# Where the normalised rows are transposed: on TensorE, or on the DMA queue of SyncE

## What is computed

```python
def _layernorm(x, axis=-1, eps=1e-05):
    m = jnp.mean(x, axis=axis, keepdims=True)
    v = jnp.var(x, axis=axis, keepdims=True)
    return (x - m) / jnp.sqrt(v + eps)

# attention: q = LN(x) @ w_q, k = ctx @ w_k, v = ctx @ w_v, causal softmax(q k^T / sqrt(512)) @ v
x = x + jnp.tanh(g_xattn[0]) * _L0_xattn_ref(_layernorm(x, axis=-1), ctx_1024, ctx_1024, w_q, w_k, w_v, 1)
# net: h = gelu(LN(x) @ ternary(W1)^T + b1), h @ ternary(W2)^T + b2
x = x + jnp.tanh(g_ffn[0]) * _L0_ffn_ref(_layernorm(x, axis=-1), W1, b1, W2, b2)
```

## Time and profile before

| | |
|---|---|
| measured, median of 3 | 1773.13 us |
| span of the profiled execution | 1771.6 us |
| TensorE matmuls busy | 1716.0 us, 97% |
| VectorE busy | 903.2 us, 51% |
| ScalarE busy | 784.0 us, 44% |
| GpSimd busy | 307.7 us, 17% |
| transposes L831 | 1024, in 128 sets of 8 |
| ScalarE copies of a set (L464, L509) | 128, about 1.02 us each |

### The profile page before, as it was taken

The page is one execution under the profiler, slowest core; times in us unless marked ns, Lnnn a source line. Parts: engine busy times, 40 slices in busy tenths (PEclk is TensorE's granted clock), DMA queues, the critical chain, the costliest instruction groups (busy, mean ns, idle before and its releaser), DMA issues.

```text
span 1771.6 us, 27014 instructions
## 1 busy us (share of the span) xinstructions
PE 1716.0 (97%) x10048; PEld 911.8 (51%) x10048; DVE 903.2 (51%) x1639; ACT 784.0 (44%) x1160; POOL 307.7 (17%) x341
## 2 busy tenths in 40 slices
PE   5799999999999999889999999999999999999999
PEld 2466656665666666555444444444444444444444
DVE  4565666666656665778443343334334434344332
ACT  2334343433343345433445544454545544554443
POOL 1111111111111111122111211122112211121110
PEclk8899999999999999999999999999999999999999
DMA  4112121121212144332110011101110111101100
GB/s 172 60 49 84 49 90 43 53 91 36 97 48 91 41 137 150 106 134 94 37 48 25 23 47 47 47 0 47 47 47 0 47 47 47 34 13 47 48 25 24
DMA packets 44570, 105.17 MB, mean 59 GB/s; under 512 B 5328, under 2 KB 5328, under 8 KB 43344
## 3 DMA queue, kind: packets, MB, share of 16 engines
q1 hardware_dynamic: 43920, 103.83, 17.5%
q10 hardware_dynamic: 576, 0.27, 0.1%
HBM read 70.53 MB, written 33.55 MB: 59 GB/s over the span
## 4 chain that ended last, share of the span: by engine, by line
PE 81%; DVE 9%; issue 7%; ACT 1%; DMA 1%; POOL 1%; DVEq 0%; SPq 0%; POOLq 0%; ACTq 0%
PE t_ps L842 12%; PE pT_ps L948 12%; PE s_ps L948 12%; PE v_ps L842 11%; PE o_ps L906 8%; PE s_ps L870 7%; PE v_ps L919 7%; PE t_ps L888 7%; PE xT_ps L831 3%; DVE v_s L797 2%; PE pT_ps L855 1%; DVE w_s L745 1%; DVE negmax L661 1%; DVE pT L652 1%; DVE ctx_s L545 1%
## 5 line engine op out<-in xcount | busy, mean ns | idle before, releaser
L771 DVE SCALAR_TENSOR_TENSOR v_s<-g,sc,v_s 128x512 f16<-128x512 f32 x256 | 233.3, 912 | 508.5 <-ACT v_s L492 506.0
L948 PE MATMUL pT_ps<-w_s,v_s 128*128 128x512 f16 x1024 | 265.5, 379 | 0.8
L948 PE MATMUL s_ps<-w_s,v_s 128*128 128x512 f16 x1024 | 262.8, 379 | 0.0
L842 PE MATMUL v_ps<-ctx_s,w_s 128*128 128x512 f16 x1024 | 241.9, 379 | 0.9 <-DVE w_s L745 0.9
L842 PE MATMUL t_ps<-ctx_s,w_s 128*128 128x512 f16 x1024 | 241.9, 379 | 0.0
L906 PE MATMUL o_ps<-v_s,pT 128*128 128x512 f16 x864 | 198.6, 381 | 9.5 <-DVE pT L652 9.5
L888 PE MATMUL t_ps<-xnT,a_s 128*128 128x256 f16 x1536 | 183.4, 277 | 23.1 <-ACT a_s L475 11.5
L870 PE MATMUL s_ps<-ctx_s,tT 128*128 128x512 f16 (+3 forms) x1152 | 197.6, 326 | 0.1
L492 ACT ACTIVATE v_s<-g,sc 128x512 f16<-128x512 f32 x256 | 184.8, 722 | 8.4
L919 PE MATMUL v_ps<-wv_s,ctx_s 128*128 128x512 f16 x768 | 178.7, 383 | 7.8 <-DVE ctx_s L545 7.8
L888 PEld LDWEIGHTS t_ps<-xnT,a_s 128*128 128x128 f16 x1536 | 151.9, 100 | 49.2 <-issue 14.4
(11 more groups left out here) (99 smaller groups left out, 1654.2 us busy)
## 6 DMA issues: line engine op xcount, KB each, us to landing
x_ring<-in_x SPq DMA_DIRECT2D x64, 256.0 KB, 2.9
raw<-in_ctxT SPq DMA_DIRECT2D x8, 2048.0 KB, 8.2
out_y<-x_ring SPq DMA_DIRECT2D x64, 256.0 KB, 3.0
raw<-out_y SPq DMA_DIRECT2D x64, 256.0 KB, 3.2
out_y<-v_s SPq DMA_DIRECT2D x64, 256.0 KB, 2.1
w_in<-in_w1T SPq DMA_DIRECT2D x16, 512.0 KB, 5.0
w_in<-in_w2T SPq DMA_DIRECT2D x16, 512.0 KB, 5.0
ctx_s<-in_wqT SPq DMA_DIRECT2D x4, 256.0 KB, 6.5
```

What stands on the lines that cost most here:

```text
L771: v.scalar_tensor_tensor(out=g_s[:, f % 4, LO], in0=g32[:, f % 2], scalar=col(C_SG), in1=g_s[:, f % 4, HI], op0=ALU.mult, op1=ALU.subtract ...
L842: last_mm = mm(h_ps[f % 2], w1_s[:, c, (f % FC) * P:(f % FC + 1) * P], yT[:, (f // FC) % 2, a, c, :], start=(a == HI and c == 0), stop=(a ...
L948: last_mm = mm(y_ps[i], g_s[:, f % 4, a, i * P:(i + 1) * P], w2_s[:, f, :], start=(f == 0 and a == HI), stop=(f == FC - 1 and a == LO))
```

## The change

The 8 transposes of a tile on PE, the PSUM tile `xT_ps` and the ACT copy go. In their place SP issues two transposing transfers a tile, one for each half, from `xn_s` (128 rows x 512 columns, f16, 128 KB) to `xnT` or `yT`. Each of the two slots of `xn_s` has a completion semaphore (`x_turned[0]`, `x_turned[1]`), which grows by 32 a tile. ACT L448 and L504 and POOL L338 and L387 now wait on it before they overwrite `xn_s`, and PE L888 and L842 wait on both before they read. In SP's slot the two transfers come first (`turn_row`), behind a wait on `t_mm` (the pair's buffer has been read) and on `xn_lo`; in a group they come behind the 4 loads and a wait that the group's first hidden matmul is done, and ahead of the 4 stores.

```diff
-        xT_ps = ps("xT_ps", [P, 2, DC, P], F16)
-        x_tr, xT_ready = sem("x_tr"), sem("xT_ready")
+        x_turned = [sem(f"x_turned{i}") for i in range(2)]
+        turn_issued, turn_free = sem("turn_issued"), sem("turn_free")
 # SyncE
+            def turn(k, r, dst):
+                sp.wait_ge(xn_lo, k + 1)
+                sp.sem_inc(turn_issued, 1)
+                for a in (HI, LO):
+                    sp.dma_start_transpose(dst[:, a], xn_s[:, r, a]).then_inc(x_turned[r], 16)
+
+            def turn_row(it, s, last=False):
+                t = it * BODY + s
+                k = t + XT_LEAD
+                if last and k >= NT:
+                    turn(k, s % 2, yT[:, 0, :, :, (k - NT) * P:(k - NT + 1) * P])
+                    return
+                if s + XT_LEAD >= 4:
+                    sp.wait_ge(t_mm, k - 2)
+                    sp.sem_inc(turn_free, 1)
+                pr, q = ((s + XT_LEAD) // 2) % 2, (s + XT_LEAD) % 2
+                turn(k, s % 2, xnT[:, pr, :, :, q * P:(q + 1) * P])
+
             def slot(it, s, last=False):
                 t = it * BODY + s
+                if not last or t + XT_LEAD < NT + GT:
+                    turn_row(it, s, last)
...
+            for s in range(-XT_LEAD, 1):
+                turn_row(0, s)
             load_ctx(1)
...
                     for i in range(GT):
                         load_x2(g * GT + GT + i, ((gg + 1) % 2) * GT + i)
+                    sp.wait_ge(h_mm, g * FC + 1)
+                    sp.sem_inc(turn_free, 1)
+                    for i in range(GT):
+                        turn(NT + GT + g * GT + i, i % 2, yT[:, (gg + 1) % 2, :, :, i * P:(i + 1) * P])
 # GpSimd, before the low half (L338; L387 alike)
-                    pool.wait_ge(x_tr, k - 1)
+                    pool.wait_ge(x_turned[r], turned_before(it, s))
 # ScalarE, before the high half (L448; L504 alike)
-                        act.wait_ge(x_tr, k - 1)
+                        act.wait_ge(x_turned[r], turned_before(it, s))
...
-                    act.wait_ge(x_tr, k + 1)
...
-                    a.activation(dst, xT_ps[:, :, :, :], ACT.Copy).then_inc(xT_ready, 1)
 # TensorE
-            def transposes(k, r):
-                pe.wait_ge(xn_lo, k + 1)
...
-                for a in (HI, LO):
-                    for c in range(DC):
-                        tr = nc.tensor.transpose(xT_ps[:, a, c], xn_s[:, r, a, c * P:(c + 1) * P], ident[:, :])
-                tr.then_inc(x_tr, 1)
             def hidden(F, f, g):
                 if f % FC == 0:
-                    pe.wait_ge(xT_ready, NT + (g + 1) * GT)
+                    for r in range(2):
+                        pe.wait_ge(x_turned[r], 16 * (NT + (g + 1) * GT))
...
-                    pe.wait_ge(xT_ready, t + T_LEAD - h + 2)
+                    for r in range(2):
+                        pe.wait_ge(x_turned[r], it * BODY * 16 + (s + T_LEAD - h + 2) * 16)
```

More of the change, by code:

```diff
@@ L217, in w_dst, with turned_before @@
             return dst[:, :, :].rearrange("p a n -> p (a n)")[:, k * WCH:(k + 1) * WCH]
+        def turned_before(it, s):
+            return it * BODY * 16 + 16 * ((s + LN_LEAD) - (s + LN_LEAD) % 2)
         LN_STEPS = (2, 4, 7, 10)
-        XT_STEPS = (4, 6, 9, 12)
         block = es.enter_context(nc.Block())
@@ L385, in group @@
                     pool.wait_ge(xn_hi, NT + tile + 1)
-                    pool.wait_ge(x_tr, NT + tile - 1)
+                    pool.wait_ge(x_turned[r], 16 * (NT + tile - i % 2))
                     g.tensor_tensor(xn_s[:, r, LO], xn32[:, r], xn_s[:, r, HI], ALU.subtract).then_inc(xn_lo, 1)
@@ L455, in slot @@
                     a.activation(v_s[:, par, HI, j], v_ps[:, :], ACT.Copy, scale=V_DOWN).then_inc(v_hi, 1)
-                if s >= -XT_LEAD and (not last or t + XT_LEAD < NT + GT):
-                    k = t + XT_LEAD
-                    act.wait_ge(x_tr, k + 1)
[L459 to L463, removed]
-                    a.activation(dst, xT_ps[:, :, :, :], ACT.Copy).then_inc(xT_ready, 1)
                 for m, n in w_turn(t, "S") if last else ():
@@ L502, in group @@
                         act.wait_ge(xn_ready, k + 1)
-                        act.wait_ge(x_tr, k - 1)
+                        act.wait_ge(x_turned[i % 2], 16 * (k - i % 2))
                         a.activation(xn_s[:, i % 2, HI], xn32[:, i % 2], ACT.Copy).then_inc(xn_hi, 1)
[L505 to L510, removed]
             hidden(0, 0)
@@ L822, in product @@
                         last_mm.then_inc(a_mm, 1)
-            def transposes(k, r):
-                pe.wait_ge(xn_lo, k + 1)
-                if not isinstance(k, int) or k > 0:
-                    pe.wait_ge(xT_ready, k)
-                for a in (HI, LO):
-                    for c in range(DC):
-                        tr = nc.tensor.transpose(xT_ps[:, a, c], xn_s[:, r, a, c * P:(c + 1) * P], ident[:, :])
-                tr.then_inc(x_tr, 1)
             def hidden(F, f, g):
                 if f % FC == 0:
-                    pe.wait_ge(xT_ready, NT + (g + 1) * GT)
+                    for r in range(2):
+                        pe.wait_ge(x_turned[r], 16 * (NT + (g + 1) * GT))
                 if f >= 2:
@@ L921, in slot @@
                     last_mm.then_inc(v_mm, 1)
-                if s >= -XT_LEAD and (not last or t + XT_LEAD < NT + GT):
-                    transposes(t + XT_LEAD, (s + XT_LEAD) % 2)
             for s in range(FIRST_SLOT, 1):
@@ L951, in group @@
                             last_mm.then_inc(y_mm, 1)
-                    if f in XT_STEPS and (not last or F + FC < NG * FC):
-                        i = XT_STEPS.index(f)
-                        transposes(NT + GT + g * GT + i, i % 2)
             with pe.Fori(0, NG // 2 - 1) as it:
```

## The result

The kernel after takes 1746.98 us (four runs, 1744.55 to 1748.82), the kernel before on the same chip 1773.25 us; the ratio is 0.9844 [0.9828, 0.9860]. The forecast was 1726.5, the range 1718 to 1762. The direction and the range held, but of the 46.7 us expected 26 to 29 came. The profiled execution of after has a span of 1742.7 us against 1771.6, a gain of 28.9 us; all that follows splits these 28.9.

The account below looks back on a forecast made before the run. TensorE, busy 97%, was taken to set the time alone in the net and most of the attention. Gains 26.7 + 18.2 + 0.9 + 0.9 = 46.7 us off 1771.6, plus 1.5, gave 1726.4, written 1726.5; range 1718 to 1762.

Parts of the forecast that it names:

- the two rivals' prices: Net: late transfers cost 15 us per us over 6.3 (chance 0.18); past 9.4, slower than before, 1780 to 1806 (0.13).
- rival A: Net: transfers land late, each us over 6.3 costs 15 us, total from 1731 to the old time; chance 0.18.
- D: Time from a tile's low half (`xn_lo`) to the landing of its second transfer; taken as about 5 us, bounds 2.7 to 9.9.
- Net, 26.7 us: Net, 1000 to 1710 us: 60 sets of 8 transposes at 0.445 us in a dense TensorE row come back, 26.7 us.
- the cover of 6.3: Net: time from the last tile's low half to the next group's first hidden matmul, less the removed set: 6.3 us.
- 120 to 700 us, 18.2 us: Attention: 48 sets give 21.4 us, less 3.2 us lost at six j = 5 places, leaving 18.2 us.
- the chain to L652 at j = 5: Attention, once a sequence: L906 waits for VectorE's copy L652; 0.24 to 0.82 us to spare against two sets, 3.2 us lost.
- Rival C: Attention: the softmax and norm chain is not shorter and takes half of the 18.2 us, giving 1735.6; chance 0.05.
- Start, 0.9 us: Before 120 us: 9 sets give nothing, ScalarE's copy L464 gone gives 1.9 us, late tile 5 costs 1.0; left 0.9 us.
- The wait for tile 5 behind the second context: Start: tile 5's transfer stands behind the 2 MB context load, some 3 us late for L888; 1.0 us lost (bounds 0 and 3).
- Weights' stage, 0.9 us: 700 to 846 us: VectorE's chain decides, the 5.64 us stall moves but stays; 2 of 11 sets, 0.9 us (bounds 0, 4.9).
- nothing is late: SyncE's queue: it waits for `o_done` most of the time, so loads and stores behind the transfers' waits are not late.

Follow-up runs that it names:

- spare: The kernel after, with four more transposing transfers that nobody reads ahead of each tile's two real ones in the net; 1807.57 us, ratio to before 1.0185.
- noturn: The kernel after with no transposing transfers, SyncE raising the same semaphores itself, transposition left out of the computation; 1734.14 us, ratio 0.9783.

## Why the prediction was right and wrong

- **The total and the range:** the direction, the net and the two rivals' prices were right. That 1746.98 lies in the range is in part luck: the forecast's own range was 1719 to 1731, and what reaches from there to 1762 is the room of rival A, a D over 6.3 us, which did not come. The time came from losses in the attention and at the start.
- **Net, 26.7 us:** right, 26.6. D was taken as 5 us and is 3.8, in its bounds; the cover of 6.3 was right (6.4 by spare), and the price of missing it too.
- **120 to 700 us, 18.2 us:** the mechanism was named, the size was not. The step that failed is that the chain to L652 at j = 5 started "at the scores two sets earlier". By the waits it started earlier: the seven waits of 11.5 us, mean 1.64, and the spare 0.35 are 2.0 us, between four and five sets a sequence and not two. The loss is 10 us and not 3.2. Rival C, held at 0.05 for want of waits in the profile of before, had the right time for this stage. The profile had the sign of it: only 0.24 to 0.82 us to spare at a place that comes once a sequence, against 8 sets of 0.445 us taken from one. The other part, 1.6 us, is PE at the turns of the loop.
- **Start, 0.9 us:** wrong, -8.2. The step that failed is the sentence that the waits of ScalarE and GpSimd on `x_turned` concern a tile that "has more than a slot". At the start there are no slots; the transfer stood in SyncE's program behind loads. With SyncE's order changed there, 7.4 of the 9.1 us came back. The wait for tile 5 behind the second context was foreseen, and L882 did wait 2.51 us. It was priced at 1.0, and the lag grew by 2.4 us from tile 1 to tile 4 (-5.8 to -8.2), part of it clock: the 24 matmuls behind that wait took 4.45 us and not 2.78.
- **Weights' stage, 0.9 us:** 0.4, within its bounds. The stall of 5.64 us moved to the product of the probabilities with v, as forecast (line below, after). Two more effects cancel: the transfers ahead of the weight loads made VectorE wait 5.9 us, and kept these loads off GpSimd's reduction.

```profile
716.59 6.17 PE L900 MATMUL o_ps<-v_s,pT 128*128 128x512 f16 x18 [5.55 <-DVE pT L653]
```

- **SyncE, "nothing is late":** right in the steady slots and in the net, wrong where loads stand behind the 2.5 us of two transfers (the last 16 slots).

## What to carry to other kernels

Work taken from the busiest engine comes back only up to the spare time of the next chain. So look, for each period of the loop, for the one place where the spare time is least, and assume that all that is removed in the period counts against it, until the trace shows where the other chain starts. A DMA put in place of engine work inherits its place in the queue's program: read what stands ahead of it in the prologue, and who waits for the buffer that it frees, not only who reads its output. And use what the change frees (here a PSUM bank) against the next bound.

## What the runs showed of the hardware

- A transposing transfer of 128x512 f16 from SBUF to SBUF took SyncE 1.25 us (a plain store or load of x mostly 0.33 to 0.43), made 544 packets, 512 of them of 256 B, and landed 2.4 us after its issue in the net. D was 3.8 us in all fifteen groups.
- In spare PE stalled 15 times for 2.9 to 3.3 us: behind eight of these stalls the granted clock fell, behind seven as long it stayed at 1.00.
- From the low half ahead of GpSimd's reduction over the partitions to the power behind it were 13.1 to 16.1 us at the same place (weights' first sum, eleven kernels), and it was longest where a weight load was issued right behind the low half. For the context's maximum it was 12.9 to 14.9.
- At the first instruction of a turn of the loop PE waited for nothing that the profile shows, 0.2 and 0.6 us without transfers and without L831 (noturn), 2.0 us in sum before, and 3.6 to 4.7 us in every kernel with transfers. That is 1.6 to 2.7 us more than before and 2.7 to 3.9 more than noturn, and I have no cause for it.
